# Causal attention with a feed-forward branch: scores made once by rows, the probabilities' halves transposed by DMA

## The chip, the cores and the metric

The kernel runs on one core of a Trainium2 chip. The time is device microseconds of one execution, as the median of several runs. The profile is that of one further execution with the hardware profiler on; all its times are in microseconds (us) unless ns is said. TensorE is PE here, VectorE DVE, ScalarE ACT, GpSimd POOL, and SyncE SP, whose queue issues all DMAs of this kernel.

## What is computed

The input x has 4 sequences of 1024 rows of 512 numbers. It is layer-normalised, goes through causal attention with 16 heads of 32 and, beside it, through a gated feed-forward net whose weights are rounded to 8 bits; both results are added to x.

```python
def attn(x, Wq, Wk, Wv, Wo):            # x: 4 x 1024 x 512, 16 heads of 32
    q, k, v = heads(x @ Wq.T), heads(x @ Wk.T), heads(x @ Wv.T)
    scores = einsum('bhqd,bhkd->bhqk', q, k) / sqrt(32)
    scores = where(tril(ones(S, S)), scores, finfo.min)
    attn = einsum('bhqk,bhkd->bhqd', softmax(scores, axis=-1), v)
    return merge(attn) @ Wo.T

def ffn(x):                             # 512 -> 1536 -> 512, weights through float8
    return qmm(silu(qmm(x, gate_w, gate_scale)) * qmm(x, up_w, up_scale), down_w, down_scale)

xn = layernorm(x)
out = x + attn(xn, Wq, Wk, Wv, Wo) + ffn(xn)
```

## The kernel before

All data are float32, and the products are made of pairs of 16-bit halves: a number is split into a high part and a low part (the number minus its high part), and PE adds up high x high, high x low and low x high.

There are two stages. `prepare` goes over 8 tiles of 512 rows: it normalises, splits and turns x, makes q, k and v of all heads and stores them as halves in DRAM (`q_dram`, `k_dram`, `v_dram`). PE is the engine that works there nearly all the time. Beside the last two tiles it also makes the maxima of heads 0 and 1 (`EARLY_MAXIMA`).

`attend` is the second stage. It has 64 heads (4 sequences of 16), four heads to an iteration (`NIT` = 16), and each head has 9 steps. Beside the four heads an iteration does the feed-forward net for 256 rows (`feed_forward`, `down`) and, from iteration 4 on (`LAG`), the output projection of 256 rows of finished attention (`project`). What each engine does in which step is written out by hand in tables (`M_STEP`, `PV_STEP`, `GATE_STEP`, `UP_STEP`, `DOWN_STEP` and others). Each engine runs through its own list in order, and semaphores hold them together.

The scores of a head are made twice:

- `maxima_scores` (L177) makes them by rows, 128 queries on the partitions, two heads ahead. `row_maxima` (L200, L205) takes the maximum of every row on DVE, with the causal mask added by DVE on the diagonal blocks. The maxima are scaled, split into halves (L214, L220, L223), turned by PE (`turn_maxima`, L230), copied (L237) and written by DMA into two spare rows of `q_st` (`store_row`, L167).
- `scores` (L1295) makes them again the other way round, 128 keys on the partitions, from `k_st` with two rows of a constant, so that the row's maximum is already taken off. ACT takes the exponential into `p32` (L1152), POOL sets the masked part of the diagonal blocks to zero (L1082), ACT casts the high half (`take_high`, L1122), and POOL, or DVE in two of nine pieces, subtracts for the low half (`take_low`, L973). In this orientation the halves `probs` are what PE needs as stationary operand for the product with v (`values`, L1308), one head later. The 33rd column of v makes the row's sum, and DVE divides (`normalise`).

A head's causal half has 36 blocks of 128x128, so 4608 columns of scores each way.

SP issues the DMAs in a fixed order (L994 loads the rows of x for the feed-forward net, L155 q and k of a head in six DMAs of 64 KB, L160 v, L1036 stores the output). One kind of DMA turns its data on the way: `turn_attention` (L1031), for the attention's halves of 128 rows, 8 blocks of 128x128 16-bit numbers (256 KB), twice an iteration.

Of the kernel before, what the change touches and what calls it, by code (L numbers as in the profile page):

```python
# [43 lines left out]
MSCALE = 1024.0  # L44
# [13 lines left out]
X_TURNED = 10  # L58

# [9 lines left out]
EARLY_MAXIMA = ({c: (2 * (c - 3), 2 * (c - 3) + 1) for c in range(3, 9)},  # L69
                {c: (2 * (c - 2), 2 * (c - 2) + 1) for c in range(2, 8)})  # L70


M_UNITS = ([(i, 0, (i + 1) * P) for i in range(4)]
           + [(i, k0, (i + 1) * P - 512 if k0 else 512)
              for i, k0 in ((4, 0), (5, 0), (4, 512), (6, 0), (5, 512), (7, 0), (6, 512), (7, 512))])

E_UNITS = [[(0, 0, 512)], [(1, 128, 384), (3, 384, 128)], [(2, 256, 256), (6, 768, 256)],
           [(0, 512, 512)], [(1, 512, 512)], [(2, 512, 512)], [(3, 512, 512)],
           [(4, 512, 512)], [(5, 640, 384), (7, 896, 128)]]
NM, NE = len(M_UNITS), len(E_UNITS)  # L80

DIAGONAL = {0: 0, 1: 384, 2: 256, 7: 0, 8: 384}
ND = len(DIAGONAL)


def p_column(j, i):

    for u, pieces in enumerate(E_UNITS):
        at = u * 512
        for key, q0, w in pieces:  # L90
            if key == j and q0 <= i * P < q0 + w:
                return at + i * P - q0
            at += w

POOL_LOW = (1, 2, 3, 4, 5, 6, 7)
DVE_LOW = tuple(u for u in range(NE) if u not in POOL_LOW)
RING = 6
FU = 3  # L100
STEPS = HEADS_PER_IT * NE


def low_parts(units, k):

    return len(units) * (k // NE) + sum(u <= k % NE for u in units)

M_STEP = {1: (0, 1), 2: (2,), 3: (3,), 4: (4,), 5: (5, 6), 6: (7, 8), 7: (9, 10), 8: (11,)}  # L110
PV_STEP = {1: (0, 1), 2: (2,), 3: (3,), 5: (4,), 6: (5,), 7: (6,), 8: (7,)}

ROW_STEP = {6: 0, 15: 1, 24: 2, 32: 3}
DOWN_STEP = {0: [(0, 0), (0, 1)], 1: [(0, 2)], 2: [(0, 3)], 3: [(0, 4)], 4: [(0, 5)],
             9: [(1, 0), (1, 1)], 10: [(1, 2)], 11: [(1, 3)], 12: [(1, 4)], 13: [(1, 5)]}
DOWN_PIECES = 6
ADD_DOWN_STEP = {5: 0, 14: 1}
# [6 lines left out]
SPLIT_STEP = {12: 0, 20: 1}  # L126
PROJ_STEP = {20: [(0, 0)], 21: [(0, 1)], 22: [(0, 2)], 28: [(1, 0)], 29: [(1, 1)], 30: [(1, 2)]}
PROJ_PIECES = 3
ADD_OUT_STEP = {23: 0, 31: 1}


def at_step(table, it, k):
# [1392 lines left out]
```

## Time and profile before

| | |
|---|---|
| median of 3 runs | 1374.51 us (1374.3 to 1374.57) |
| the profiled execution, whole | 1372.59 us |
| its span | 1370.9 us |
| busy: PE, DVE, ACT, POOL | 1305.0, 1071.2, 929.3, 956.3 us |
| packets of the DMA queue of SP | 123.67 MB, 33.2% of 16 engines' span |
| stage `prepare` | about 315 us |
| stage `attend` | about 1055 us |

Busy time is what an engine spends in instructions of its own; the busy time of PE has the modelled end of the last of a row of pipelined matmuls in it. The granted clock is full (1.00 of 2.4 GHz) in all of the second stage but its first 15 us. The share of the DMA engines is the mean over 16 of them.

### The profile page before, as it was taken

The page shows a single profiled execution, that of the slowest core. Times are in us where ns is not written, and L with a number is a line of the kernel's source. Part 1 is how long each engine was busy: PE and PEld are TensorE (multiplying, and loading weights), DVE is VectorE, ACT ScalarE, POOL GpSimd, SP SyncE. Part 2 cuts the span into 40 slices and gives each one's busy share as a digit, 9 for nine tenths or more (in the row PEclk, how much of TensorE's full clock was granted, in tenths as well). Part 3 has the DMA queues.
Part 4 walks back from the last instruction along what each step waited for, and adds up shares of the span by engine and source line. Part 5 has one row for each costly group of instructions (what it writes and reads, how often), then busy time and mean ns, then how long its engine had stood idle before and what let it go on. Part 6 is the DMA issues. An engine that isn't in the chain of part 4 may idle for free.

```text
span 1370.9 us, 33729 instructions
## 1 busy us (share of the span) xinstructions
PE 1305.0 (95%) x12062; PEld 843.9 (62%) x12062; DVE 1071.2 (78%) x2870; ACT 929.3 (68%) x1766; POOL 956.3 (70%) x1304
## 2 busy tenths in 40 slices
PE   4899999897999999999999999999999999999987
PEld 2444445444666666676766667676767676666754
DVE  7777878877878787887878787878788787878763
ACT  3333333226878788887878887887878787878851
POOL 1322222205889888898988888888989898888863
PEclk9999999998999999999999999999999999999999
DMA  7278766543122121222323231313222232312131
GB/s 257 85 201 217 212 189 190 159 147 79 54 58 64 33 64 41 71 56 72 79 56 91 51 87 41 86 48 89 56 76 56 71 79 58 95 46 86 41 71 62
DMA packets 141753, 125.83 MB, mean 92 GB/s; under 512 B 52434, under 2 KB 110034, under 8 KB 141586
## 3 DMA queue, kind: packets, MB, share of 16 engines
q1 hardware_dynamic: 141586, 123.67, 33.2%
q8 instruction: 96, 1.57, 0.5%
q14 instruction: 71, 0.58, 0.1%
HBM read 74.86 MB, written 42.21 MB: 85 GB/s over the span
## 4 chain that ended last, share of the span: by engine, by line
PE 64%; DVE 6%; ACT 3%; issue 2%; POOL 1%; DMA 0%; ACTq 0%; SPq 0%; DVEq 0%
PE bank L1330 20%; PE bank L1344 12%; PE bank L1308 9%; PE bank L177 8%; PE bank L1295 8%; PE bank L1361 6%; DVE ga L1232 1%; ACT th L1129 1%; DVE junk L200 1%; DVE mx L205 1%; DVE probs L973 1%; ACT p L1152 1%; DVE fu L1237 1%; ACT probs L1122 1%; PE bank L230 1%
## 5 line engine op out<-in xcount | busy, mean ns | idle before, releaser
L1152 ACT ACTIVATE p<-bank,s_exp 128x512 f32<-128x512 f32 x576 | 396.3, 688 | 186.6 <-PE bank L1295 178.9
L973 POOL TENSOR_TENSOR probs<-p,probs 128x512 f16<-128x512 f32 x448 | 514.2, 1158 | 0.6 <-ACT probs L1122 0.6
L1122 ACT CAST probs<-p 128x512 f16<-128x512 f32 x576 | 352.1, 611 | 0.1
L1082 POOL TENSOR_SCALAR_AFFINE_SELECT p<-p 128x256 f32<-128x256 f32 (+1 forms) x320 | 152.0, 475 | 126.8 <-ACT p L1152 126.7
L205 DVE TENSOR_REDUCE mx<-bank 128x1 f32<-128x512 f32 x264 | 180.2, 686 | 73.6 <-PE bank L177 68.8
L177 PE MATMUL bank<-k_st,q_st 96*128 96x512 f16 (+3 forms) x792 | 221.6, 328 | 15.1 <-DVE mx L205 9.3
L1308 PEld LDWEIGHTS bank<-v_sb,probs 128*128 128x128 f16 x4608 | 198.1, 97 | 51.7 <-issue 1.6
L1295 PE MATMUL bank<-q_st,k_st 98*128 98x512 f16 (+3 forms) x768 | 221.2, 329 | 6.2 <-PEq L252 4.6
L1308 PE MATMUL bank<-v_sb,probs 128*128 128x65 f16 x4608 | 213.9, 192 | 2.6 <-DVE attn L1199 2.6
L1330 PE MATMUL bank<-xt,wg 128*128 128x256 f16 x1536 | 200.2, 273 | 5.9 <-DVE fu L1237 5.6
L1330 PE MATMUL bank<-xt,wu 128*128 128x256 f16 x1536 | 199.6, 273 | 0.0
L1344 PE MATMUL bank<-wd,fuse 128*128 128x512 f16 x768 | 190.6, 378 | 0.9 <-DVE ff_out L1225 0.9
L857 PE MATMUL bank<-x_t,w_t 128*128 128x512 f16 x768 | 171.5, 382 | 2.0 <-issue 1.6
L200 DVE CUSTOM_DVE_ANT_0 junk<-bank,mask,mx 128x128 bf16<-128x128 f32 (+3 forms) x264 | 143.3, 543 | 25.1 <-PE bank L177 25.0
L1330 PEld LDWEIGHTS bank<-xt,wg 128*128 128x128 f16 x1536 | 141.0, 98 | 34.9 <-DVE fu L1237 7.5
L1330 PEld LDWEIGHTS bank<-xt,wu 128*128 128x128 f16 x1536 | 142.2, 98 | 24.1 <-issue 0.3
L1069 POOL TENSOR_TENSOR fuse<-fu,fuse 128x256 f16<-128x256 f32 x192 | 142.7, 743 | 12.8 <-ACT fuse L1137 12.8
L200 DVE CUSTOM_DVE_ANT_0 junk<-bank,mask 128x128 bf16<-128x128 f32 (+3 forms) x264 | 123.2, 486 | 30.9 <-PE bank L177 30.8
L857 PEld LDWEIGHTS bank<-x_t,w_t 128*128 128x128 f16 x768 | 74.8, 98 | 94.1 <-issue 5.0
L177 PEld LDWEIGHTS bank<-k_st,q_st 96*128 96x128 f16 x792 | 74.8, 98 | 92.5 <-DVE mx L200 24.9
L1232 DVE SCALAR_TENSOR_TENSOR ga<-th,bank 128x256 f32<-128x256 f32 x192 | 80.1, 417 | 52.2 <-ACT th L1129 52.2
L531 ACT CAST qk_st<-bank 128x512 f16<-128x512 f32 x64 | 37.5, 586 | 121.5 <-PE bank L857 121.4
(114 smaller groups left out, 1612.7 us busy)
## 6 DMA issues: line engine op xcount, KB each, us to landing
q_st<-q_parts SPq DMA_DIRECT2D x201, 64.0 KB, 2.1
k_st<-k_parts SPq DMA_DIRECT2D x201, 64.0 KB, 2.0
v_sb<-v_parts SPq DMA_DIRECT2D x66, 132.0 KB, 2.2
xt<-xn_parts SPq DMA_DIRECT2D x17, 512.0 KB, 4.6
v_parts<-res SPq DMA_DIRECT2D x8, 1056.0 KB, 7.1
x_in<-in_L_attn_x SPq DMA_DIRECT2D x8, 1024.0 KB, 6.3
xn_parts<-x_t SPq DMA_DIRECT2D x16, 512.0 KB, 6.6
q_parts<-qk_st SPq DMA_DIRECT2D x32, 256.0 KB, 3.9
```

Of the source, the lines that this page charges most:

```text
L177: nc.tensor.matmul(banks[u % len(banks)][:, 0:w], rows.q_st[i][part, blk * P:(blk + 1) * P], rows.k_st[i][part, k0:k0 + w], start=True, st ...
L200: ins = nc.vector.tensor_tensor_reduce(out=rows.junk[u % 2][:, 0:w], in0=src, in1=rows.mask[:, 512 - w:512], scale=1.0, scalar=at if k0 el ...
L205: ins = nc.vector.tensor_reduce(at, src, AX.X, ALU.max)
L857: mm = nc.tensor.matmul(bank[2 + c % 4][:, :], lhs, rhs, start=first, stop=((wp, xp) == TERMS[-1] and kc == KC - 1))
L973: ops.tensor_tensor(probs[s % 2][:, LO, at], p32[k % RING][:, :], probs[s % 2][:, HI, at], ALU.subtract).then_inc(signal, 1)
L1082: nc.gpsimd.affine_select(out=at, in_=at, compare_op=ALU.is_ge, fill=0.0, base=0, pattern=[[0, blocks], [1, P]], channel_multiplier=-1).th ...
L1122: nc.scalar.copy(probs[s % 2][:, HI, u * 512:(u + 1) * 512], p32[k % RING][:, :]).then_inc(p_hi, 1)
L1152: nc.scalar.activation(p32[k % RING][:, :], st_bank[(s + u) % 2][:, :], ACT.Exp, scale=s_exp[:, :]).then_inc(exp_done, 1)
L1295: mm = nc.tensor.matmul(st_bank[(s + u) % 2][:, at:at + w], k_st[s][:, j * P:(j + 1) * P], q_st[s][:, q0:q0 + w], start=True, stop=True)
L1308: mm = nc.tensor.matmul(o_half[:, i % (QB // 2), :], probs[s % 2][:, part, at:at + P], v_sb[s][:, j, 0:VN], start=(j == 0 and part == HI), ...
L1330: mm = nc.tensor.matmul(ff_bank[f % 2][:, h * FT:(h + 1) * FT], (wg8, wu8)[h][:, kc, f * P:(f + 1) * P], xt[:, part, kc, :], start=(part = ...
L1344: mm = nc.tensor.matmul(misc[:, :], fuse[:, part, f, i * P:(i + 1) * P], wd8[:, f, :], start=(f == 0 and part == HI), stop=(f == FC - 1 an ...
```

## The change

- PE makes the scores once, by rows (queries on the partitions), with the plain halves of q and k. The rows of a head are put together in 5 groups: block row 7; 6 and 0; 5 and 1; 4 and 2; 3 (`GROUPS`), 1024 columns each but the last, which has 512. A head has 10 steps instead of 9. A group's scores take a pair of PSUM banks, and there are two pairs.
- PE adds the mask to the 8 diagonal blocks with a matmul of an identity and a 128x128 mask (L1244 of the kernel after).
- DVE takes the maximum over each whole row of the group (one reduction for each block row, 8 a head) and multiplies it by a negative factor; ACT takes the exponential with this as its bias. The affine select, the turning of maxima and all that belongs to it are gone, and so are the early maxima of `prepare`.
- ACT casts the high half and POOL (DVE for group 4) subtracts for the low half, into one of four buffers `p16`. Since queries are now on the partitions, a DMA turns both halves of a group into `p_t`, from which PE makes the product with v as before. SP issues these DMAs, five a head, four with 16 blocks of 128x128 and one with 8.
- q and k lie in DRAM with their halves side by side for each head, so a head is loaded by four DMAs instead of six. Storing them takes four DMAs of 64 KB each where there was one of 256 KB.
- The tables of steps are rewritten for 10 steps a head.

```diff
-M_UNITS = ([(i, 0, (i + 1) * P) for i in range(4)]
-           + [(i, k0, (i + 1) * P - 512 if k0 else 512)
...
+GROUPS = ((7,), (6, 0), (5, 1), (4, 2), (3,))
+NG = len(GROUPS)
+WIDTH = [sum(i + 1 for i in rows) * P for rows in GROUPS]
...
+PV_ROWS = {1: (7,), 3: (6,), 4: (5,), 5: (4,), 7: (3, 2), 8: (1, 0)}
+POOL_LOW = (0, 1, 2, 3)
+P32_RING, P16_RING, MX_RING = 3, 4, 4
-GATE_STEP = {4: 0, 6: 1, 8: 2, 14: 3, 16: 4, 18: 5, 19: 6, 23: 7, 25: 8, 27: 9, 31: 10, 33: 11}
-UP_STEP = {5: 0, 7: 1, 13: 2, 15: 3, 17: 4, 18: 5, 22: 6, 24: 7, 26: 8, 27: 9, 31: 10, 34: 11}
+GATE_STEP = {7: 0, 9: 1, 14: 2, 17: 3, 19: 4, 20: 5, 26: 6, 28: 7, 29: 8, 35: 9, 37: 10, 39: 11}
+UP_STEP = {8: 0, 9: 1, 17: 2, 18: 3, 19: 4, 21: 5, 27: 6, 29: 7, 30: 8, 36: 9, 38: 10, 39: 11}
 SWIGLU_STEP = {k + 2: f for k, f in UP_STEP.items()}
...
-                    sp.dma_start(dst[ds(t // 2, 1), ds(t % 2, 1), c % 4].rearrange("b u p w t -> p (b u w) t"),
-                                 qk_st[c][:, :, :]).then_inc(qk_stored[c], 16)
+                    for a in range(4):
+                        sp.dma_start(dst[first + a, :, :, at].rearrange("w d t -> d w t"),
+                                     qk_st[c][a * DK:(a + 1) * DK, :, :]).then_inc(qk_stored[c], 16)
...
+            def turn_scores(n, g):
+                e = NG * n + g
+                owned, signal = (POOL_LOW, p_lo_pool) if g in POOL_LOW else (DVE_LOW, p_lo_dve)
+                sp.wait_ge(signal, low_groups(owned, e + 1))
+                wait(sp, pv_mm, 2 * (n - 1))
+                w = 2 * WIDTH[g]
+                sp.dma_start_transpose(p_t[n % 2][:, PT_AT[g]:PT_AT[g] + w].rearrange("p (b t) -> p b t", t=P),
+                                       p16[e % P16_RING][:, 0:w]).then_inc(p_turned[e % P16_RING], 16)
...
+            def exponentials(e):
+                g = e % NG
+                act.wait_ge(neg_set, e + 1)
+                wait_low(act, e + 1 - P32_RING)
+                for r, i in enumerate(GROUPS[g]):
+                    at = slice(first_column(i), first_column(i) + (i + 1) * P)
+                    last = nc.scalar.activation(p32[e % P32_RING][:, at], pair[e % 2][:, at], ACT.Exp,
+                                                bias=m_neg[:, e % MX_RING, r:r + 1], scale=s_exp[:, :])
+                last.then_inc(exp_done, 1)
+            def take_high(e):
...
+                act.wait_ge(exp_done, e + 1)
+                wait(act, p_turned[e % P16_RING], 16 * (e // P16_RING))
+                nc.scalar.copy(parts_of(e, HI), p32[e % P32_RING][:, 0:WIDTH[e % NG]]).then_inc(p_hi, 1)
...
+            def maxima(e):
...
+                for r, i in enumerate(GROUPS[g]):
+                    at = slice(first_column(i), first_column(i) + (i + 1) * P)
+                    last = nc.vector.tensor_reduce(mx[:, e % MX_RING, r:r + 1], pair[e % 2][:, at], AX.X, ALU.max)
...
+            def scores(n, g):
+                e, s = NG * n + g, n % HEAD_RING
...
                 wait(pe, exp_done, e - 1)
...
+                out = pair[e % 2]
+                for i, k0, at, w in pieces_of(g):
+                    nc.tensor.matmul(out[:, at:at + w], q_st[s][:, i * P:(i + 1) * P], k_st[s][:, k0:k0 + w],
+                                     start=at % 512 == 0, stop=at == 0 and WIDTH[g] > 512)
+                for at in diagonal(g):
+                    mm = nc.tensor.matmul(out[:, at:at + P], rows.ident_bf[:, :], rows.mask[:, :], start=False,
+                                          stop=at == diagonal(g)[-1])
```

SP's order for two heads of an iteration with an output projection, before. `q_st<-m_row` is the row of maxima, `a_t<-a_part` the transpose of the attention rows, and the last number of the shapes of a transpose is the block's width.

```order
L1031 DMA_TRANSPOSE a_t<-a_part 128x8x128
L155 DMA q_st<-q_parts 32x1024 x3
L155 DMA k_st<-k_parts 32x1024 x3
L160 DMA v_sb<-v_parts 128x528
L1036 DMA out<-o_sb 128x512
L1017 DMA res<-in_L_attn_x 128x2x512
L167 DMA q_st<-m_row 2x8x128
L994 DMA xt<-xn_parts 128x2048
```

The same queue after, for one head and the start of the next (`p_0` to `p_3` are the four buffers `p16`).

```order
L170 DMA q_st<-q_parts 64x1024
L172 DMA q_st<-q_parts 32x1024
L170 DMA k_st<-k_parts 64x1024
L172 DMA k_st<-k_parts 32x1024
L921 DMA_TRANSPOSE p_t<-p_1 128x16x128
L928 DMA_TRANSPOSE a_t<-a_part 128x8x128
L177 DMA v_sb<-v_parts 128x528
L921 DMA_TRANSPOSE p_t<-p_2 128x16x128
L921 DMA_TRANSPOSE p_t<-p_3 128x16x128
L921 DMA_TRANSPOSE p_t<-p_0 128x16x128
L921 DMA_TRANSPOSE p_t<-p_1 128x8x128
```

The loads stay, two fewer; the row of maxima is gone, and five transposes a head stand between them, the one of the attention rows behind the first.

PE's order at the start of a head beside the feed-forward net's `down`, before.

```order
L177 MATMUL bank<-k_st,q_st 128x128
L177 MATMUL bank<-k_st,q_st 128x256
L1308 MATMUL bank<-v_sb,probs 128x65 x6
L1344 MATMUL bank<-wd,fuse 128x512 x4
L1295 MATMUL bank<-q_st,k_st 128x256 x2
L177 MATMUL bank<-k_st,q_st 128x384
L1308 MATMUL bank<-v_sb,probs 128x65 x6
L1344 MATMUL bank<-wd,fuse 128x512 x4
L1295 MATMUL bank<-q_st,k_st 128x512
L177 MATMUL bank<-k_st,q_st 128x512
```

After, the same place: scores of group 0, then of group 1, each with its masks (`pair<-mask,ident_bf`).

```order
L1241 MATMUL pair<-k_st,q_st 128x512 x2
L1244 MATMUL pair<-mask,ident_bf 128x128
L1297 MATMUL bank<-wd,fuse 128x512 x4
L1261 MATMUL bank<-v_sb,p_t 128x65 x16
L1297 MATMUL bank<-wd,fuse 128x512 x4
L1241 MATMUL pair<-k_st,q_st 128x512
L1241 MATMUL pair<-k_st,q_st 128x384
L1241 MATMUL pair<-k_st,q_st 128x128
L1244 MATMUL pair<-mask,ident_bf 128x128 x2
```

PE no longer alternates between two kinds of scores; the masks come as extra matmuls of 128 columns, and the product with v begins with the longest row.

## Rows read from the trace of the kernel before

**Rows 1.** Busy time by window, each about one iteration of the second stage.

```profile
core 0: us, PE busy (x) PEld busy (x) DVE busy (x) ACT busy (x) POOL busy (x), PEclk, DMA share, GB/s
...
436.60:498.30 61.70, 58.56 (x630) 41.33 (x629) 49.59 (x150) 50.62 (x100) 53.29 (x71) 1.00 0.19 53
560.00:623.50 63.50, 62.92 (x654) 43.80 (x653) 50.98 (x152) 51.67 (x102) 55.85 (x74) 1.00 0.26 69
623.50:687.00 63.50, 62.92 (x655) 43.78 (x654) 50.98 (x152) 51.68 (x102) 55.59 (x73) 1.00 0.29 69
```

**Rows 2.** The xt loads, one an iteration: count, duration in ns, first and last start.

```profile
L994 SPq DMA_DIRECT2D xt<-xn_parts x17: 322/328/338, 319.7 to 1321.7; - x17
```

**Rows 3.** Groups by line and shape, 623.5:687: count, busy us, mean ns, idle before.

```profile
L973 POOL TENSOR_TENSOR probs<-p,probs 128x512 f16<-128x512 f32 x28 | 32.1, 1157 | 0.0
L1152 ACT ACTIVATE p<-bank,s_exp 128x512 f32<-128x512 f32 x36 | 24.8, 688 | 11.8 <-PE bank L1295 11.3
L1122 ACT CAST probs<-p 128x512 f16<-128x512 f32 x36 | 22.0, 611 | 0.0
...
L205 DVE TENSOR_REDUCE mx<-bank 128x1 f32<-128x512 f32 x16 | 11.0, 687 | 4.7 <-PE bank L177 4.4
L1069 POOL TENSOR_TENSOR fuse<-fu,fuse 128x256 f16<-128x256 f32 x13 | 9.6, 740 | 0.5 <-ACT fuse L1137 0.5
...
L1295 PE MATMUL bank<-q_st,k_st 98*128 98x512 f16 x24 | 9.2, 381 | 0.0
...
L973 DVE TENSOR_TENSOR probs<-p,probs 128x512 f16<-128x512 f32 x8 | 6.2, 772 | 0.0
...
L1237 DVE SCALAR_TENSOR_TENSOR fu<-bank,c_ff,ga 128x256 f32<-128x256 f32 x12 | 5.8, 484 | 0.4
L1129 ACT ACTIVATE th<-bank,half_gs 128x256 f32<-128x256 f32 x12 | 5.7, 474 | 0.0
...
L1137 ACT CAST fuse<-fu 128x256 f16<-128x256 f32 x12 | 4.9, 406 | 0.0
```

**Rows 4.** PE in order of time: start us, us, instructions.

```profile
346.56 1.04 PE L1330 MATMUL bank<-xt,wg 128*128 128x256 f16 x8
347.44 1.04 PE L1330 MATMUL bank<-xt,wu 128*128 128x256 f16 x8
```

**Rows 5.** The SP queue in order of time, 716:752: start us, us issuing.

```profile
717.11 1.26 SPq L1031 DMA_TRANSPOSE a_t<-a_part  x1
718.41 1.50 SPq L155 DMA_DIRECT2D q_st<-q_parts  x3
...
722.17 0.42 SPq L160 DMA_DIRECT2D v_sb<-v_parts  x1
...
733.73 2.08 SPq L1031 DMA_TRANSPOSE a_t<-a_part  x1
...
750.42 0.33 SPq L994 DMA_DIRECT2D xt<-xn_parts  x1
```

**Rows 6.** All transposes of the kernel before: issue ns min/median/max, and landing.

```profile
L1031 SPq DMA_TRANSPOSE a_t<-a_part x24: 1249/1257/2114, 590.1 to 1305.0; - x24
...
DMA to landing us min/median/max: 3.1/3.2/5.3
```

**Rows 7.** The windows view for one microsecond of a transpose, columns as in Rows 1.

```profile
591.00:592.00 1.00, 1.00 (x22) 0.81 (x20) 0.95 (x3) 0.96 (x3) 1.00 (x3) 1.00 0.59 118
```

**Rows 8.** Page, part 3: the queue that fetches instructions, packets and MB.

```profile
q8 instruction: 96, 1.57, 0.5%
```

**Rows 9.** PE in the preparation; then two windows, columns as in Rows 1.

```profile
289.40 0.33 PE L177 MATMUL bank<-k_st,q_st 96*128 96x128 f16 x2
289.56 2.75 PE L857 MATMUL bank<-x_t,w_t 128*128 128x512 f16 x12
...
315.00:320.00 5.00, 0.44 (x2) 0.14 (x2) 3.40 (x14) 0.47 (x1) 0.00 (x0) 0.71 0.58 168
335.00:340.00 5.00, 3.50 (x36) 2.18 (x37) 4.93 (x13) 4.88 (x11) 4.88 (x8) 1.00 0.13 38
```

## What I predict, and how it follows

> **What bounds the kernel now.** I read the windows view first, cut at the xt loads, of which there is one an iteration [rows 2]. From the fifth iteration on, an iteration takes 63.5 us and PE is busy for 62.9 of them at full clock, while DVE is busy 51, ACT 52, POOL 56 us and the DMA engines 26 to 29% [rows 1]. So PE sets the time of twelve of the sixteen iterations. The first four have no output projection. They take 61.7 us (the very first 55, which I take from the first start of the loads and the mean spacing), with PE busy 58.6 [rows 1, 2]. There PE also waits for others, by some 3 us. The groups of one iteration say what PE does [rows 3]; its real price is the distance between starts: eight matmuls of 256 columns start 0.88 us before the next eight, 110 ns each [rows 4]. The 381 ns shown for 512 columns of scores [rows 3] include the pipeline's end; by the spacing they cost about 215.
>
> **PE.** A head has 36 blocks of 128x128 scores under or on the diagonal, 4608 columns. Before, they are made twice (L177 and L1295): 2 x 4608 columns at 0.43 ns are 2 x 1.98 us a head, 15.8 us an iteration, and with the turning of the maxima (4 of them, some 0.15 each) 16.4. After: 1.98 us a head once, and 8 masks of 128 columns, 8 x 0.055 = 0.44. That is 9.7 us. PE needs 63.5 - 16.4 + 9.7 = 56.8 us. The tables of steps put gates 4 and 8 of the feed-forward into the step in which DVE does the swiglu that they need; in the step before PE has about 1.1 us of work (8 matmuls of 110 ns, and values), DVE a maximum of 0.69, its negation and the swiglu's two operations of about 0.48 each, with hops 1.9 [rows 3], so I add 2 x 0.8 us: **58.4 us**.
>
> **ACT, DVE, POOL.** ACT's exp has 688 ns for 512 columns and tanh 474 for 256, so 0.84 a column and about 260 fixed; the casts 611 and 406, so 0.80 and 200 [rows 3]. After, a head has 8 exps and 5 casts over 4608 columns: 5.9 + 4.7 us, against 6.2 + 5.5. DVE: 4608 columns of maximum cost at most 4608/512 x 687 ns = 6.2 us a head, in 8 instructions now and in 12 before; five tiny negations of perhaps 0.2 each come, and one subtraction of 772 ns goes [rows 3]. POOL: the subtraction has 1157 ns for 512 columns and 740 for 256, so 1.63 a column and 325 fixed; four of 1024 columns make 8.0 us a head where seven of 512 made 8.1, and the ten affine selects of diagonals go. ACT and POOL get shorter by 1 us a head or more, DVE by some 0.5 to 1. None becomes the bound: they were at most 56 of 63.5 us.
>
> **The SP queue and the DMA engines** take what was removed. A head's halves are 72 blocks. The existing transpose moves 8 blocks (256 KB) and keeps the queue for 1257 ns (median of 24), with the next issue 1.30 us after its own [rows 5, 6]. Is that the price of 8 blocks, or a fixed price of an instruction? The microsecond inside a transpose shows the 16 DMA engines at 92% at 189 GB/s [rows 7], and 256 KB at that rate are 1.35 us: the engines are full, so I scale by blocks. That gives per iteration:
> - 36 units of 8 blocks for the probabilities and 2 for the attention rows: 38 x 1.257 = 47.8 us.
> - 16 head loads, each like the three q loads that issue in 1.50 us, 0.45 taken: 7.2; 4 v loads of 0.42: 1.7; res, xt and two stores at about 0.4: 1.6 [rows 5].
> - 46 instructions with about 0.05 us between them (717.11 + 1.26 to 718.41 is 0.04): 2.3.
>
> The sum is **60.6 us**, already over PE's 58.4. Then disturbances: one transpose of the 24 took 2114 ns, another 2.08 us [rows 5, 6]. I see 5 of 24 like these in the timeline, 0.8 us longer each. If that share holds, 38 x 5/24 x 0.8 = 6.3 us are added. If instead it is the instruction fetches, of which 96 fall into 1371 us [rows 8], thus 4.4 into an iteration, 4.4 x 0.8 = 3.5. I add 4.4: **65.0 us**. The engines' own time says the same: the share times the window is 16.5 to 18.4 us an iteration [rows 1], less two transposes 14 to 16; with 38 x 1.257 that is 62 to 64 us at a share of 1. Bounds for the queue: 60.6 undisturbed, 68 with all terms at their upper end.
>
> Who waits: SP issues in order, and PE's products with v wait for the landing of a head's halves. The cast of a group waits for the transpose four groups earlier (a ring of four 16-bit buffers), so a late queue holds back ACT, then the maxima, then PE. The landing itself (3.2 us [rows 6], some 4.5 for 16 blocks) is hidden: PE uses a group nine to eleven steps of ten a head after its scores, 14 us or more, and from scores to landing I count 0.5 + 1.4 + 1.1 + 1.0 + 2.0 + 4.5 = 10.5 us. If the cover goes, that is the third rival.
>
> The Trainium skill speaks against this pricing. DMA: Bandwidth & Descriptors, "Latency and other measured facts", gives a DMA transpose 350 to 400 GB/s when contiguous and 261 otherwise; this case's trace shows 189. An estimate by that page: 38 x 256 KB at 375 GB/s are 26.6 us, the queue would stay near 42 us, and PE would bind; that is the second rival's result. The measured rate decides here, since the form of the instruction is the same.
>
> **Preparation and ends.** The 24 early matmuls of maxima stand between PE's projections, 289.40 to 289.56 the first two of them [rows 9]; 24 at about 0.17 are 4 us, and PE idles there for some 3 us on maxima. Both go: -7. The eight stores of q and k of a tile become 32, 24 more issues of 0.45, 11 us on a queue with 33 us a tile; hidden by PE's projections. At the start the first group needs no row, so a little less; at the end the last transposes have a late queue ahead of them, up to 5 us. I take +3 for the end and +3 for the first iteration, which was 55 us long and now starts the queue.
>
> **Sum.** Twelve iterations: 12 x (65.0 - 63.5) = +18. Iterations two to four: no attention rows, no stores, so 65.0 - 2 x 1.3 - 2 x 0.4 = 61.6 against 61.7: 0. First +3, end +3, preparation -7. Together +17 us on the profiled execution's 1372.6 (its span is 1370.9), so 1389.6. The median of the runs is 1374.5, 1.9 higher: I say **1391 us**.
>
> **The rivals.**
> 1. The queue is the bound, but less disturbed than the few transposes of before suggest: 61.5 us an iteration. 12 x (-2) + 3 x (-3.6) + 1 + 3 - 7 = -38: 1336 us. For it: the ring can take up a hiccup when engines are full anyway. Against: 5 of 24 were late with the queue two thirds idle.
> 2. The transposes run faster back to back than alone; PE binds at 58.4: 12 x (-5.1), the first four at about 56, 4 x (-4), -7: about -85, 1290 us. Against it stand the full engines [rows 7]. PE's clock need not suffer from short waits: at 70% busy it was still full, and it fell to half only after 4.6 us of idling [rows 9].
> 3. Slower by more: a bubble in the ring of four. Between the end of one issue and the turn of its successor's successor in the same buffer, three transposes pass, 6.3 us in the worst place. Landing (2.0 after the issue), cast 1.0, subtraction 2.0 and the hops 0.6 make 5.6. One tanh or fuse (0.5 to 0.75) ahead of them on ACT or POOL breaks it; from there on each head loses about 1 us: 16 x 4 = +64 on top, 1455 us. If transposes even waited for each other's landing, a head would take 4 x 4.5 + 3.2 = 21 us and the kernel some 330 us more.
>
> **How the numbers follow.** Forecast case, 1377 to 1425: 0.36. Third rival: 0.22. Within 0.2%, which is about what a measurement of this kernel can tell from no change (an iteration of 64.0): 0.05. First rival and what lies between it and no change: 0.27. Second: 0.10. Faster 0.37, same 0.05, slower 0.58. The range leaves out the second rival, and most of the third: 1315 to 1435. The case of slower alone runs from 1377 to 1435.
>
> **What would show it.** In the profile after: the DMA share near 1 in the second stage, SP issuing almost without a gap, PE's idle time ending on transposes (waits of the products with v, or of the scores on exps that stand behind a late cast); an issue of 16 blocks near 2.5 us. A DMA share near 0.7 with PE at 97% would be the second rival. A DMA share of 0.8 with PE at 80% would be the third, or a wait that I haven't seen. Wrong above all would be the price of a transpose of 16 blocks, which no row shows.

## The result, and the profile after

The kernel after takes 1492.6 us (median of 4 runs, 1488.9 to 1500.7), the one before 1374.5 (4 runs): 1.087 times as long, with a 95% interval of 1.085 to 1.089. The forecast had the direction, but +17 us where +118 came, and the time lies outside its range. The profiled execution's span is 1489.5 us against 1370.9.

First the page of the kernel after: engines, the DMA share in 40 slices of the span, the DMA queue, the chain that ended last, and five groups of instructions (busy us, mean ns | idle before, releaser).

```profile
PE 1249.0 (84%) x11844; PEld 820.3 (55%) x11845; DVE 1126.3 (76%) x2250; ACT 934.5 (63%) x1381; POOL 811.8 (54%) x663
...
DMA  7278866667989899988999898979798979898961
...
q1 hardware_dynamic: 740208, 272.47, 83.0%
...
DVE 21%; PE 20%; issue 14%; ACT 11%; DMA 6%; SPq 4%; POOL 4%; ACTq 0%; DVEq 0%; POOLq 0%
...
L1047 ACT ACTIVATE p<-pair,m_neg,s_exp 128x1024 f32<-128x1024 f32 (+7 forms) x512 | 404.5, 828 | 227.1 <-DVE m_neg L1127 226.8
L890 POOL TENSOR_TENSOR p<-p,p 128x1024 f16<-128x1024 f32 x191 | 406.0, 2130 | 92.9 <-ACT p L1058 92.9
...
L1275 PE MATMUL bank<-xt,wg 128*128 128x256 f16 x1536 | 218.3, 289 | 110.5 <-DVE fu L1181 110.5
...
L1261 PE MATMUL bank<-v_sb,p_t 128*128 128x65 f16 x4608 | 202.1, 194 | 48.1 <-DMA p_t<-p 39.8
...
L1127 DVE TENSOR_SCALAR m_neg<-mx,s_neg 128x2 f32<-128x2 f32 (+1 forms) x320 | 175.7, 549 | 11.3
```

PE is busy for 84% of the span where it was 95, and no other engine has taken its place. The DMA queue's share went from 33 to 83% of the span, near to what was forecast. But the chain that ended last gives the DMA engines and the SP queue only 10% together; DVE and PE have 41, and "issue" (time for which the profile shows no wait) 14. PE's longest idle time does not end on a transpose. It ends on `fu` of the swiglu (110.5 us before the gates, L1275), and only then come the values (L1261), with 39.8 on transposes. And the negation of a row's maximum (L1127), two numbers for each partition, takes 549 ns on average, where the prediction had 0.2 us.

Two iterations of the kernel after and two long windows of its second stage, columns as in [rows 1]:

```profile
869.80:940.40 70.60, 58.51 (x644) 41.44 (x643) 54.63 (x117) 52.32 (x80) 46.60 (x33) 0.98 0.97 195
940.40:1013.30 72.90, 60.66 (x639) 42.53 (x638) 54.76 (x115) 51.51 (x78) 46.21 (x32) 0.93 0.90 189
500.00:900.00 400.00, 334.44 (x3589) 237.78 (x3590) 313.08 (x659) 294.63 (x441) 263.34 (x181) 0.94 0.94 192
900.00:1300.00 400.00, 329.31 (x3549) 232.45 (x3548) 307.73 (x645) 288.30 (x434) 255.55 (x177) 0.95 0.90 190
```

The iterations with an output projection take 70.6 to 73.3 us, mean 71.9, against 63.5 [rows 1] and a forecast of 65.0. The DMA engines' share is high (0.90 to 0.97), which looks like the forecast's bound. The granted clock is no longer 1.00.

And the loads of xt and the transposes of the probabilities (duration ns min/median/max):

```profile
L910 SPq DMA_DIRECT2D xt<-xn_parts x16: 343/574/576, 307.7 to 1373.5; - x16
...
L921 SPq DMA_TRANSPOSE p_t<-p x320: 1232/1734/6142, 314.8 to 1443.8; - x160
...
DMA to landing us min/median/max: 2.7/4.0/9.4
```

With [rows 2] this says where the +118 us of the span stand. The first xt load starts at 307.7 where it was 319.7: -12, the preparation. The first four iterations take 275.1 us where they took 240.3: +35. The next eleven take 790.7 against 698.2: +92. From the sixteenth load to the end it is 116.0 us against 112.7: +3.

### The profile page after: what moved, and what is told of

Read it like the earlier page. It is cut to its first block, busy times and chain, and to the rows that moved or that the text cites. A ratio compares the mean times of both kernels' runs of the same rounds, so it can differ in the third digit from the quotient of the medians.

```text
span 1489.5 us, 31583 instructions
## 1 busy us (share of the span) xinstructions
PE 1249.0 (84%) x11844; PEld 820.3 (55%) x11845; DVE 1126.3 (76%) x2250; ACT 934.5 (63%) x1381; POOL 811.8 (54%) x663
## 4 chain that ended last, share of the span: by engine, by line
DVE 21%; PE 20%; issue 14%; ACT 11%; DMA 6%; SPq 4%; POOL 4%; ACTq 0%; DVEq 0%; POOLq 0%
PE bank L1275 10%; DVE mx L1123 9%; ACT p L1047 7%; DMA p_t<-p 6%; DVE m_neg L1127 6%; POOL p L890 3%; PE pair L1241 3%; SPq L921 3%; ACT p L1058 2%; DVE ga L1176 2%; ACT th L1065 2%; PE bank L1297 2%; PE bank L1261 2%; PE pair L1314 1%; PE bank L1314 1%
## 5 line engine op out<-in xcount | busy, mean ns | idle before, releaser
L1047 ACT ACTIVATE p<-pair,m_neg,s_exp 128x1024 f32<-128x1024 f32 (+7 forms) x512 | 404.5, 828 | 227.1 <-DVE m_neg L1127 226.8
L890 POOL TENSOR_TENSOR p<-p,p 128x1024 f16<-128x1024 f32 x191 | 406.0, 2130 | 92.9 <-ACT p L1058 92.9
L1123 DVE TENSOR_REDUCE mx<-pair 128x1 f32<-128x1024 f32 (+7 forms) x512 | 367.8, 749 | 116.0 <-PE pair L1244 114.8
L1058 ACT CAST p<-p 128x1024 f16<-128x1024 f32 (+1 forms) x320 | 307.4, 961 | 9.2 <-DMA p_t<-p 3.7
L1275 PE MATMUL bank<-xt,wg 128*128 128x256 f16 x1536 | 218.3, 289 | 110.5 <-DVE fu L1181 110.5
L1261 PE MATMUL bank<-v_sb,p_t 128*128 128x65 f16 x4608 | 202.1, 194 | 48.1 <-DMA p_t<-p 39.8
L1261 PEld LDWEIGHTS bank<-v_sb,p_t 128*128 128x128 f16 x4608 | 181.7, 98 | 98.5 <-DMA p_t<-p 33.2
L1241 PE MATMUL pair<-k_st,q_st 96*128 96x512 f16 (+3 forms) x896 | 188.7, 316 | 49.8 <-ACT p L1047 45.0
L1275 PEld LDWEIGHTS bank<-xt,wg 128*128 128x128 f16 x1536 | 146.3, 103 | 146.4 <-DVE fu L1181 123.6
L1275 PE MATMUL bank<-xt,wu 128*128 128x256 f16 x1536 | 225.5, 296 | 0.0
L890 POOL TENSOR_TENSOR p<-p 128x1024 f16<-128x1024 f32 x65 | 138.2, 2129 | 91.9 <-ACT p L1058 91.9
L1127 DVE TENSOR_SCALAR m_neg<-mx,s_neg 128x2 f32<-128x2 f32 (+1 forms) x320 | 175.7, 549 | 11.3
L1275 PEld LDWEIGHTS bank<-xt,wu 128*128 128x128 f16 x1536 | 157.0, 107 | 30.9 <-issue 3.6
L1065 ACT ACTIVATE th<-bank,half_gs 128x256 f32<-128x256 f32 x192 | 90.7, 473 | 72.8 <-PE bank L1275 72.8
L1181 DVE SCALAR_TENSOR_TENSOR fu<-bank,c_ff,ga 128x256 f32<-128x256 f32 x192 | 92.9, 484 | 6.8
```

What stands on the lines that cost most here:

```text
L890: ops.tensor_tensor(parts_of(e, LO), p32[e % P32_RING][:, 0:WIDTH[e % NG]], parts_of(e, HI), ALU.subtract).then_inc(signal, 1)
L1047: last = nc.scalar.activation(p32[e % P32_RING][:, at], pair[e % 2][:, at], ACT.Exp, bias=m_neg[:, e % MX_RING, r:r + 1], scale=s_exp[:, :])
L1058: nc.scalar.copy(parts_of(e, HI), p32[e % P32_RING][:, 0:WIDTH[e % NG]]).then_inc(p_hi, 1)
L1065: nc.scalar.activation(th[f % 2][:, :], ff_bank[f % 2][:, 0:FT], ACT.Tanh, scale=half_gs[:, f:f + 1]).then_inc(tanh_done, 1)
L1123: last = nc.vector.tensor_reduce(mx[:, e % MX_RING, r:r + 1], pair[e % 2][:, at], AX.X, ALU.max)
L1127: nc.vector.tensor_scalar(m_neg[:, e % MX_RING, 0:count], mx[:, e % MX_RING, 0:count], s_neg[:, 0:1], None, ALU.mult).then_inc(neg_set, 1)
```

## The experiments

Two theories stood at the start. **Q** (the prediction's): the SP queue and the DMA engines behind it bind, and the rest are consequences. **L**: DVE's tiny negation is held up by POOL, this delays ACT's exponentials and all that stands behind them in ACT's order, the swiglu too, and PE stalls. Beside them **G**: the tables' two tight gates alone make PE's stalls. Times are medians; ratios are to the kernel before, measured on the same chip (1374.2 to 1374.9 us each time), with 95% intervals.

### Where L comes from: the negation ends when POOL does

The stretch from 904 to 917 of the kernel after, by engine in order of time (start us, us; in brackets the idle time before and what ended it). POOL, then DVE, ACT, PE:

```profile
903.97 2.14 POOL L890 TENSOR_TENSOR p<-p 128x1024 f16<-128x1024 f32 x1
...
907.81 4.22 POOL L890 TENSOR_TENSOR p<-p,p 128x1024 f16<-128x1024 f32 x2
```

```profile
905.47 0.67 DVE L1127 TENSOR_SCALAR m_neg<-mx,s_neg 128x2 f32<-128x2 f32 x1
...
908.96 1.01 DVE L1127 TENSOR_SCALAR m_neg<-mx,s_neg 128x2 f32<-128x2 f32 x1
...
910.60 0.21 DVE L1127 TENSOR_SCALAR m_neg<-mx,s_neg 128x1 f32<-128x1 f32 x1
...
913.40 0.48 DVE L1181 SCALAR_TENSOR_TENSOR fu<-bank,c_ff,ga 128x256 f32<-128x256 f32 x1
```

```profile
910.01 1.45 ACT L1047 ACTIVATE p<-pair,m_neg,s_exp 128x640 f32<-128x640 f32 x2 [1.08 <-DVE m_neg L1127]
911.49 1.04 ACT L1058 CAST p<-p 128x1024 f16<-128x1024 f32 x1
912.44 0.47 ACT L1065 ACTIVATE th<-bank,half_gs 128x256 f32<-128x256 f32 x1
```

```profile
908.91 1.04 PE L1275 MATMUL bank<-xt,wg 128*128 128x256 f16 x8
913.94 1.89 PE L1275 MATMUL bank<-xt,wg 128*128 128x256 f16 x8 [4.00 <-DVE fu L1181]
915.62 1.79 PE L1275 MATMUL bank<-xt,wu 128*128 128x256 f16 x8
```

POOL's subtraction of 903.97 ends at 906.11 (the next ones, 907.81 for two, at about 909.94 and 912.03). The negation of 905.47 ends at 906.14 and the one of 908.96 at 909.97: each about 30 ns after POOL. The one of 910.60, of one column, takes 0.21 us in the middle of a POOL instruction. Over the whole trace, 118 of the 192 negations of two columns take over 260 ns, and all 118 end 21 to 29 ns after the end of a POOL instruction; those that meet no POOL instruction take about 0.23 us. Of the 128 of one column none takes over 260 ns, and 60 of them run wholly inside a POOL instruction. By form, 860 to 1010:

```profile
L1127 DVE TENSOR_SCALAR m_neg<-mx,s_neg 128x2 f32<-128x2 f32 x24 | 17.2, 718 | 0.8
...
L1127 DVE TENSOR_SCALAR m_neg<-mx,s_neg 128x1 f32<-128x1 f32 x17 | 3.6, 214 | 0.6
```

This agrees with the Trainium skill, "SBUF — State Buffer", section "Who interferes with whom": a DVE operation in a mode that uses both ports, and any POOL operation, use one shared pair of ports, the first of the two holds it for its whole instruction, and the other one blocks; tensor_scalar can be such an operation, tensor_reduce can't. "VectorE: DVE Perf Modes", section "Mode 2×_2P — use both read ports for one tensor", makes that mode depend on an outermost size over 1 that is even (or the same in source and destination). Two columns meet it, and one does not. The runs show when a negation ends and how long it takes; the ports themselves no run shows.

What follows in the window: the exponentials wait 1.08 us for the negation, their cast comes next in ACT's order, then the tanh that the swiglu needs at 912.44, the swiglu at 913.40, and PE, whose gate waits for a bank, has idled for 4.00 us at 913.94. Then eight matmuls of 256 columns start 1.68 us before the next eight, instead of 0.88 [rows 4]: half clock.

Not all of the 4.00 us is the negation's. It took 1.01 us where an undisturbed one takes 0.23, so 0.8 us of this stall are its wait for POOL. The rest is the exponentials (1.45) and the cast (1.04) that stand ahead of the tanh in ACT's order, and the swiglu behind it.

### One negation a column: e1_neg1

```diff
-                nc.vector.tensor_scalar(m_neg[:, e % MX_RING, 0:count], mx[:, e % MX_RING, 0:count], s_neg[:, 0:1], None,
-                                        ALU.mult).then_inc(neg_set, 1)
+                for r in range(count):
+                    last = nc.vector.tensor_scalar(m_neg[:, e % MX_RING, r:r + 1], mx[:, e % MX_RING, r:r + 1],
+                                                   s_neg[:, 0:1], None, ALU.mult)
+                last.then_inc(neg_set, 1)
```

> The negation of the maxima is issued one column at a time (two instructions of 128x1 where there was one of 128x2); all else as in the kernel after. Theory L (lock): in the kernel after 118 of the 192 two-column negations end 21 to 29 ns after a POOL instruction ends, none of the one-column ones does; they hold 108 us beyond 0.21 us each, and they stand in the chain scores, maximum, negation, exp, scores. L expects all negations at 0.21 us and 1410 to 1450 us. Theory Q (the DMA queue binds): the wait goes and the time stays, 1480 to 1495. Theory G (gates in the step of their swiglu): 1480 or above too, since PE still waits for the swiglu.

Measured: 1430.6 us, 1.041 [1.038, 1.044], 62 us less than the kernel after. L holds. DVE makes 512 negations where it made 320, and they keep it 84 us less. The group of all negations, and below it PE's wait for `fu` in 500:1300 (us in total, times, longest), in this kernel:

```profile
L1128 DVE TENSOR_SCALAR m_neg<-mx,s_neg 128x1 f32<-128x1 f32 x512 | 91.6, 210 | 11.3
```

```profile
PE bank L1277 <- DVE fu L1183: 75.9, 35, 3.2
```

It isn't all: PE's wait before the gates is hardly less than the 80.5 us of the kernel after, of which the next experiment shows the row. The longest fell from 4.0 to 3.2 us, by the 0.8 worked out above.

### The gates apart: e2_gates

```diff
-GATE_STEP = {7: 0, 9: 1, 14: 2, 17: 3, 19: 4, 20: 5, 26: 6, 28: 7, 29: 8, 35: 9, 37: 10, 39: 11}
-UP_STEP = {8: 0, 9: 1, 17: 2, 18: 3, 19: 4, 21: 5, 27: 6, 29: 7, 30: 8, 36: 9, 38: 10, 39: 11}
+GATE_STEP = {7: 0, 9: 1, 14: 2, 17: 3, 20: 4, 22: 5, 25: 6, 27: 7, 30: 8, 32: 9, 35: 10, 37: 11}
+UP_STEP = {8: 0, 9: 1, 16: 2, 18: 3, 21: 4, 23: 5, 26: 6, 28: 7, 31: 8, 33: 9, 36: 10, 38: 11}
```

> Only the tables of gate and up steps change, so that each gate comes two steps after the swiglu that it waits for (before: gates 4 and 8 in the same step, gate 5 too). G expects PE's waits for the swiglu (110 us in the kernel after) to go down to under 20 and the time to fall by 40 to 90 us, to 1400 to 1450. Q expects 1480 to 1495. L expects a small gain, 1475 to 1495, since the negations still wait for POOL.

Measured: 1473.5 us, 1.071 [1.068, 1.074], 19 us less, 1.5 below L's range and far from G's. Waits in 500:1300 of after, then of e2_gates (us in total, times, longest):

```profile
PE bank L1275 <- DVE fu L1181: 80.5, 33, 4.0
...
PE pair L1241 <- ACT p L1047: 21.6, 17, 3.7
```

```profile
PE pair L1241 <- ACT p L1047: 36.5, 25, 2.7
...
PE bank L1275 <- DVE fu L1181: 9.5, 17, 0.6
```

71 us of stalls before the gates went in these 800 us (and 15 came at the scores, which wait for exponentials), and 19 us of the whole kernel: the gates were the place where PE waited, and mostly not the reason.

### Half of the transposes: e3_half

The product takes the high halves of the probabilities twice, and only they are turned: 8 and 4 blocks instead of 16 and 8, same instructions otherwise.

```diff
-                w = 2 * WIDTH[g]
+                w = WIDTH[g]
...
-                        at = block_column(j, i, part)
+                        at = block_column(j, i, HI)
```

> Half the volume of the transposes: only the high halves are turned (16 blocks become 8, 8 become 4), and the product with v takes them twice, so the low halves of the probabilities are missing from the result; instructions and waits are the same in number. Q expects a large gain, to under 1430 us, with a DMA share near 0.5. L and G expect the share to fall and the time to stay within 20 us of 1493.

Measured: 1466.4 us, 1.066 [1.062, 1.070], 26 us less, so beyond the 20 of L and G too, but far from Q's. Halving what was forecast to be the bound gives a fifth of the loss back. The window 500:900 and the transposes of this kernel:

```profile
500.00:900.00 400.00, 338.70 (x3707) 240.97 (x3706) 321.34 (x680) 302.84 (x456) 271.35 (x188) 0.96 0.61 129
...
L921 SPq DMA_TRANSPOSE p_t<-p x320: 1188/1242/2512, 315.6 to 1421.6; - x160
```

With the DMA engines at 0.61 an iteration still takes 69.7 us on average. So in the kernel as changed, Q is not the main thing that holds it.

### Both together, and then half: e4_neg_gates, e5_neg_gates_half, e6_neg_half

e4 has the edits of e1 and e2; e5 those of e1, e2 and e3; e6 those of e1 and e3.

> Both edits, one-column negations and the moved gates. If L and G hold: 1370 to 1420 us, by what the queue allows; by my estimate of 65 us an iteration of queue time it stops at about 1390. Q alone expects 1480 to 1495.

> All three edits: one-column negations, moved gates, and only the high halves turned (the low halves of the probabilities are missing from the result). The kernel with the first two stands at 1422 us with a DMA share of 0.97 to 1.02. Theory Q2 (with the two other causes gone the queue binds at 66 to 69 us an iteration) expects 1300 to 1350 us here, near PE's own 58 us an iteration. The rival (the rest is still the chain maximum, negation, exp, cast) expects 1390 to 1420.

> One-column negations and only the high halves turned (the low halves of the probabilities are missing from the result); the gates as in the kernel after. The kernel with the negations alone stands at 1431 us with a DMA share of 0.97 to 1.03. Q2 expects a gain of 30 us or more on it, and less than in the kernel with moved gates, since PE's 80 to 100 us of waits for the swiglu stay: 1360 to 1400. If the queue doesn't bind even there: 1415 to 1430.

Measured: e4 1422.5 us, 1.035 [1.032, 1.037], 2.5 us above its range. e5 1370.8, 0.997 [0.996, 0.999], between the range of Q2 and that of its rival. e6 1381.0, 1.005 [1.004, 1.007], as Q2 had it. The two windows of e4, and the first of e5:

```profile
500.00:900.00 400.00, 343.23 (x3816) 244.89 (x3816) 304.14 (x770) 313.65 (x470) 278.74 (x192) 0.98 1.02 204
900.00:1300.00 400.00, 348.63 (x3775) 246.25 (x3775) 297.55 (x750) 305.23 (x458) 273.47 (x189) 0.96 0.97 202
```

```profile
500.00:900.00 400.00, 357.17 (x4059) 256.59 (x4057) 319.26 (x812) 327.70 (x496) 294.87 (x203) 1.00 0.68 141
```

Halving the volume is worth 26 us with the lock there, and 50 (e1 to e6) or 52 (e4 to e5) without it. So once the negation is free, the volume is the dearest thing left, at a share of the DMA engines of 1.02 and 0.97 in e4 and an iteration of 67.6 us. That is the bound that the prediction named, with two limits. The gain of 52 was less than the 72 or more that Q2 asked for. And a share of 1.00 is no ceiling, since it adds up the times of packets: 20 us of e4 show 1.22.

```profile
600.00:620.00 20.00, 17.80 (x213) 13.59 (x211) 15.07 (x39) 14.94 (x25) 13.21 (x11) 1.00 1.22 210
```

Halving the volume also lets each transpose land earlier (2.8 us in the median in e3_half, 4.0 in the kernel after), and no run separates the two. The losses overlap, too: the gates are worth 19 alone, 8 after the negation, 10 after negation and volume.

### POOL's instructions cut in two: e7_pool_split

If the wait is for the POOL instruction that happens to run, half as long a one must halve the longest wait, with the negation left as it is.

```diff
-            ops.tensor_tensor(parts_of(e, LO), p32[e % P32_RING][:, 0:WIDTH[e % NG]], parts_of(e, HI),
-                              ALU.subtract).then_inc(signal, 1)
+            for at in range(0, WIDTH[e % NG], 512):
+                last = ops.tensor_tensor(parts_of(e, LO)[:, at:at + 512], p32[e % P32_RING][:, at:at + 512],
+                                         parts_of(e, HI)[:, at:at + 512], ALU.subtract)
+            last.then_inc(signal, 1)
```

> The kernel after with POOL's subtraction in two instructions of 512 columns instead of one of 1024 (0.3 us more work each time); the negations stay two columns wide on DVE. If a negation waits for the POOL instruction that is under way (theory L), the longest waits go from about 2.1 us to about 1.1, the mean of the negations from 549 ns to 350 to 450, and the time falls by 10 to 40 us, to 1450 to 1480. If the long negations have another cause, their mean stays at 549 and the time is 1493 or more.

Measured: 1469.4 us, 1.070 [1.068, 1.072]. All negations of this kernel, then two groups of it:

```profile
L1129 DVE TENSOR_SCALAR m_neg<-mx,s_neg x320: 212/228/1229, 308.1 to 1411.1; 128x2 f32<-128x2 f32 x96, 128x1 f32<-128x1 f32 x64
```

```profile
L891 POOL TENSOR_TENSOR p<-p,p 128x512 f16<-128x512 f32 x382 | 433.2, 1157 | 70.3 <-ACT p L1060 69.1
...
L1129 DVE TENSOR_SCALAR m_neg<-mx,s_neg 128x2 f32<-128x2 f32 (+1 forms) x320 | 144.1, 450 | 11.3
```

The longest negation went from 2174 ns, one POOL instruction of 2130 and a little, to 1229, one of 1157 and a little. The mean fell by 99 ns to 450, and the time by 23 us. The time and the mean lie where L had them (the mean at its edge). Together with the ends of the negations this shows what they wait for.

### What is left: e8_neg_gates_pv and e9_neg_gates_pv_half

A further theory, **O**: the first values of a head wait until DVE's last operation on the head before has left the one bank of sums. e8 is e4 with the values of block row 7 one step later (`PV_ROWS` 1: (7,) becomes 2: (7,)). e9 is e8 with the halved volume.

> The kernel with one-column negations and moved gates (1422 us), with the first row of the product with v one step later (step 2 instead of 1 of a head). In the kernels before this one PE waits there 0.7 to 1.6 us a head, until DVE's last operation on the previous head has left the one PSUM bank of the sums (theory O). If the queue binds here as theory Q2 says, the wait only moves to the transposes: 1405 to 1425. If O is a cause of its own here, up to 60 us go: 1360 to 1400.

> The same with only the high halves turned (the low halves of the probabilities are missing from the result); without the moved row this kernel stands at 1371 us. O expects its 50 to 70 us of waits to go: 1310 to 1345. If the chain through ACT binds instead, the time stays within 15 us of 1371.

Measured: e8 1415.1 us, 1.031 [1.029, 1.032]; e9 1358.2, 0.989 [0.987, 0.991]. Both times are what was expected if O is no large cause. With the volume as it is, the later place is worth 7 us (13 with it halved), and PE waits for the transposes as before, 45.8 us where it was 40.4 in e4 (first fence: e8's window 500:900; second: its waits in 500:1300). Third, waits in 500:1300 of e9:

```profile
500.00:900.00 400.00, 350.10 (x3848) 249.08 (x3849) 304.43 (x778) 315.02 (x473) 282.57 (x193) 0.97 1.01 208
```

```profile
PE bank L1263 <- DMA p_t<-p: 45.8, 21, 4.5
```

```profile
PE pair L1243 <- ACT p L1047: 30.5, 53, 1.0
...
PE bank L1263 <- DVE attn L1145: 24.3, 25, 1.3
```

The window 500:900 of e9:

```profile
500.00:900.00 400.00, 362.74 (x4113) 260.70 (x4111) 320.87 (x817) 331.13 (x500) 297.73 (x205) 1.00 0.67 142
```

PE is busy for 90.7% at full clock; its iterations there are 62.4 us long, so its work is 56.6 us. The other 5.8 show as many short waits (for exponentials before the scores and for DVE's division before the values, as above; 12.4 us in 500:1300 for transposes and 10.7 for the swiglu), the longest of them 2.0 us. Which of them would have to go for PE to be the bound was not tried, and stays open. e9 is 1.1% faster than the kernel before, but it leaves out the low halves; without halving, nothing here reaches the kernel before.

### PE turns a group: e10_pe_turns_g4, e11_pe_turns_g4_late, and its control e12_low_on_pool

If the volume is the bound, PE can take some of it. In e10 (from e8) PE turns group 4 with 8 transposes of 128 columns into the unused half of the pair of banks, DVE copies the result to `p_t`, and POOL makes its subtraction. The scores of group 1 use that pair next and wait for the copy. e11 puts those scores behind the first row of values. e12 has only POOL's subtraction.

```diff
+            def turn_g4(n):
...
+                for b in range(2 * WIDTH[4] // P):
+                    mm = nc.tensor.transpose(dst[:, b, :], src[:, b * P:(b + 1) * P], ident[:, :])
+                mm.then_inc(g4_mm, 1)
...
+            def copy_g4(n):
...
+                nc.vector.tensor_copy(p_t[n % 2][:, PT_AT[4]:PT_AT[4] + 2 * WIDTH[4]],
+                                      pair[e % 2][:, 512:1024].bitcast(F16)).then_inc(g4_copied, 1)
...
+                if g == 1:
+                    wait(pe, g4_copied, n)
...
-                    turn_scores(n, 4)
```

> On the kernel with one-column negations, moved gates and moved row (1415 us): group 4 of each head (8 of its 72 blocks) is turned by PE into the unused half of its PSUM pair and copied by DVE, its subtraction goes from DVE to POOL; the queue has four transposes a head instead of five, nothing is missing from the result. Q2 (the queue binds there): 4 x 1.25 us less an iteration, 1335 to 1375 us, faster than the kernel before if nothing else takes over. Rival (the chain through the PSUM pair binds): scores of group 1 now wait for the copy, 1400 to 1430.

> The same with the scores of group 1 behind the first row of the product with v, which gives the copy 0.5 us more before they wait for it. If that wait matters: 5 to 25 us less than the run before it. If not, or if it delays DVE's maxima: the same or up to 10 us more.

> The kernel of 1415 us (one-column negations, moved gates, moved row) with the one subtraction a head that DVE still does (group 4, 0.68 us, in front of which DVE has the next group's maximum) given to POOL (1.15 us). It was part of the two kernels in which PE turns group 4. If the chain through DVE counts, 5 to 20 us faster; if the queue sets the time and POOL hands over as early, within 5 us of 1415. If this edit explained their 1602 and 1543 us, it would be over 1450.

Measured: e10 1601.8 us, 1.165 [1.163, 1.166]; e11 1543.0, 1.122 [1.120, 1.125]; e12 1411.6, 1.027 [1.025, 1.028], so the subtraction's engine is worth 3.5 us, within the 5 that were expected if the queue sets the time, and it doesn't explain e10 and e11. e10 lies above both of its ranges. e10, 800:816, in order of time:

```profile
805.50 1.03 PE L1297 MATMUL pair<-ident,p 128*128 128x128 f16 x8 [3.70 <-POOL p L896]
806.58 0.69 DVE L1198 COPY p_t<-pair 128x1024 f16<-128x1024 f16 x1 [2.49 <-PE pair L1297]
...
807.41 1.01 PE L1263 MATMUL pair<-k_st,q_st 96*128 96x512 f16 x3 [0.88 <-DVE p_t L1198]
```

PE's turn waits 3.70 us for the end of the chain of group 4 (scores, maximum, negation, exponential, cast, subtraction), DVE 2.49 for PE, and PE 0.88 for DVE. The window 500:900 of e10:

```profile
500.00:900.00 400.00, 320.65 (x3436) 230.14 (x3434) 255.78 (x652) 267.67 (x399) 256.94 (x182) 0.92 0.74 157
```

The DMA share has fallen to 0.74, from e8's 1.01, and all engines do less in 400 us; an iteration is longer by 187 us / 16 = 11.7 against e8. e11, with the scores of group 1 behind the first row of values, gets 59 us of it back where at most 25 were expected. This is the opposite of what was expected of e10: a fifth row of transposes, which PE met late only now and then (45.8 us of 800 for all of them in e8), was replaced by work that PE must wait for in the middle of its order. In 500:1300 of e10 the waits before the turns alone come to 98.4 us.

## Why the prediction was wrong, point by point

**The tiny negations: the step that failed.** "Five tiny negations of perhaps 0.2 each", a price with no row behind it, and no bound from above. One column does take 0.21 us. Those of two columns take up to 2.17 and 0.77 on average, because they wait for POOL, whose instruction the same change made 2.13 us long. Freed, they give 62 us back (e1_neg1), more than any other edit by itself, and the 1430.6 us that are left lie inside the predicted range. The prediction priced each engine by itself and said that none becomes the bound. This remained true of their sums (DVE 76%), but it was no argument for the path: maximum, negation, exponential, cast, and in ACT's order the tanh behind them, now stand between PE's scores and the next release of a pair or a bank, and a late negation delays them all. The 226.8 us that the exponentials wait for it are not the price of this: the row has in it the wait for the maximum ahead, and with the negations freed it still shows 174.5 us (e1_neg1) and, in a kernel faster by 70 us, 226.5 (e4).

**The gates: right place, wrong size.** 0.8 us was taken for each of gates 4 and 8. Single stalls reach 4.0 us, since the hops were summed undisturbed; DVE and ACT had the late chain ahead of the swiglu. The gates by themselves are worth 19 us where the prediction had 16 x 1.6 = 26 as PE's need, none of it in its sum, since the queue bound there.

**The DMA engines: right as a bound, but second in line.** Priced by blocks, an iteration was to take 65.0 us, at most 68. The kernels without the first two causes give 67.6 (e4) and 67.2 (e8) at a share of 0.97 to 1.02, and the volume is then worth 50 to 57 us. e8's 1415 us lies in the case's own 1377 to 1425. In the kernel after the volume is worth 26.

The price was read from the wrong row. [rows 7] has a share of 0.59 and 118 GB/s; the 92% and 189 GB/s stand in the microsecond behind it, when the next loads had been issued too:

```profile
592.00:593.00 1.00, 1.00 (x10) 0.80 (x9) 0.97 (x5) 0.50 (x1) 1.00 (x2) 1.00 0.92 189
```

So "the engines are full" was weakly founded, and no row gave the price of 16 blocks, as the prediction says itself. An estimate from e8 and e9: the share times the iteration falls from about 0.99 x 67.2 to 0.66 x 63.0 us for 18 units of 8 blocks less, so 1.4 us a unit where 1.257 was taken. By that the undisturbed sum is near 66 and not 60.6, and it was luck that the 4.4 added for disturbances covered most of the difference.

**The SP queue: wrong place for the same price.** An issue of 16 blocks was to hold SP for 2.5 us, and SP was to issue almost without a gap. The median of all 320 issues is 1.73 us, 64 of them of 8 blocks; the shortest of 16 blocks is 1.32, hardly more than the 1.23 of 8. And SP waits. Its waits in 500:1300, of the kernel after and of e4:

```profile
SPq L921 <- POOL p L890: 143.6, 102, 3.3
SPq L921 <- DVE p L890: 38.3, 15, 4.1
```

```profile
SPq L921 <- POOL p L890: 118.8, 95, 2.8
SPq L921 <- DVE p L890: 9.9, 12, 1.2
```

For 182 of 800 us SP had nothing to issue, since the subtraction was not done; in e4, with the engines at a share of 1, for 129. The engines carry on with what was issued before. So what there is of a bound at 65 us and more belongs to the engines, and the queue could have taken more. This was the row to look for in the result: a queue that waits for somebody isn't the bound.

**PE: right.** 56.8 us of work an iteration were worked out and 56.6 are measured (e9, full clock). But "PE's clock need not suffer" failed: the stalls grew long enough, and the mean granted clock of the execution is 0.947 where it was 0.991; in e9, without long stalls, it is 0.986. The rows warned, with half clock after 4.6 us of idling [rows 9].

**Preparation and ends: right in sign.** -12 instead of -7 at the first xt load; +3 at the end, as predicted. The first four iterations, priced at +3 together, took +35, 8.7 us each, where the later ones took 8.4: what was lost does not depend on the output projection, nor on the attention rows' transposes, which the first four don't have.

**The rivals.** The first (61.5 us an iteration, undisturbed) and the second (PE binds at 58.4) fall with the rates: with the full volume and the engines at a share of 1, all DMA traffic came to 204 and 208 GB/s (e4, e8). The Trainium skill's 350 to 400 GB/s ("DMA: Bandwidth & Descriptors", section "Latency and other measured facts") are not seen here: all traffic together, averaged over 400 us, stays at 208 at most. The third had the right form, a wait that isn't a sum of busy times, in the wrong place. Its broken ring of four would show as casts that wait for transposes, and these are 3.7 us in the whole kernel after:

```profile
ACT p L1058 <- DMA p_t<-p: 3.7, 7, 1.2
```

With transposes half as long, 92 of the 118 us are still there (e3_half). The prediction's last part came close to the profile that followed ("A DMA share of 0.8 with PE at 80% would be the third, or a wait that I haven't seen"), but it gave that wait neither a price nor a chance. One count of work was wrong without effect: five affine selects a head go from POOL, not ten (L1082 of the kernel before, 320 for 64 heads).

**The balance**, one after the other, from 1492.6: negation -62, gates then -8, later values -7, POOL -3.5, to 1411.6. 37 us are left to the kernel before. The volume alone is worth more than that (-57 between e8 and e9), so in this order the transposes' volume is what stands between the change and a gain. It was halved there by leaving out the low halves; no run here has the whole result, less volume and a time below the kernel before.

## What to carry to other kernels

When a change gives DVE even a tiny operation on SBUF with two columns or more (two are what was measured here), look at what POOL runs beside it and how long one of its instructions is; make it one column at a time, or cut POOL's instruction. When the sum of each engine says that none binds, walk the path of one unit through all engines in their order as well, and price what stands ahead of it in each queue at its worst, not its mean. An engine that waits in the middle of its order for a chain can be dearer than a transfer that is sometimes late (here by 187 us).

## What the runs showed of the hardware

- A tensor_scalar of 128x2 float32 numbers takes 0.23 us when no POOL instruction runs and up to 2.17 beside POOL, 0.77 on average; of 128x1 always 0.20 to 0.22, even in the middle of a POOL instruction. Two of one column are cheaper here than one of two.
- Transposes by DMA from SBUF to SBUF: the issues of the kernel after (four of 16 blocks to one of 8) have a median of 1.73 us, those of e3_half (four of 8 to one of 4) 1.24, so twice the blocks don't hold the issuing queue twice as long. The median time from issue to landing is 4.0 and 2.8 us. Meanwhile all DMA traffic together came to 201 to 208 GB/s at a share of 0.97 to 1.02 (e4, e8).
- After a stall of 4.00 us, PE's matmuls came at half clock: eight of 256 columns in 1.68 us instead of 0.88 at full clock [rows 4].
